# Pausing the gather queue with a short memset, and gathering one group of fields in two blocks: a DLRM tower on one core

## The chip, the cores and the metric

The kernel runs on one core of one Trainium2 chip. The metric is the device time of one execution in microseconds (us), as the median over several runs. Differences of about 1% are what a measurement of this kernel can tell.

## The reference

For 2048 samples, 40 embedding rows of 32 floats are looked up (one table per field, 1000 to 125000 rows each). Every pair of the 40 fields is joined by its own 32x32 matrix (780 pairs), and the 780 results and 16 dense values go through a three-layer perceptron.

```python
e = jnp.stack([tbl_f[ids[:, f]] for f in range(40)], axis=1)            # 2048 x 40 x 32
iidx, jidx = jnp.triu_indices(40, k=1)
z = jnp.einsum('bpd,pde,bpe->bp', e[:, iidx], bilinear_matrices, e[:, jidx])
h = jnp.concatenate([z, dense_ctx], axis=1)                             # 2048 x 796
h = jnp.maximum(h @ W_top1 + b_top1, 0.0)                               # 512
h = jnp.maximum(h @ W_top2 + b_top2, 0.0)                               # 256
y = h @ W_top3                                                          # 2048 x 1
```

## The kernel before

The batch is cut into 4 blocks of 512 samples, the fields into 10 chunks of 4 fields (128 partitions, feature by sample). A block has 50 units, one for each pair of chunks (and five "twin" units for pairs within chunks), and one cycle g works one unit, so the kernel has 200 cycles, 50 for each block. In a cycle TensorE projects a chunk with the pair matrices into PSUM (`project`, L935, L944), VectorE multiplies that with the other chunk (`multiply`, L823 and its like, two multiplications of 128x1024 in a cycle), and TensorE sums the products into `bank_z` (`sum_up`, L960). The sum of cycle g-1 stands behind the projection of cycle g+1 in TensorE's queue.

The embeddings come in two ways.

- Gathered: GpSimd issues indirect DMAs (L586), each of 128 rows of 128 bytes, so 4 for a field and block. They land in `rows`, a ring of 7 slots, one slot for a chunk and block (a "turn"). TensorE transposes the four tiles of a turn (`turn`, L909) once the turn's semaphore has all its landings, and ScalarE copies the result to `x_T` (`keep_turn`, L631). GpSimd goes through the turns in order. It waits for a slot (`turned`), for a due cycle of each field (`DUE`, by `summed`, 0.8 blocks ahead in order), and after every fourth gather (`BURST = 4`) for the landing of the gather just issued (L593).
- Looked up: 16 fields with small tables are multiplied out. Their tables stand in SBUF, split in three bf16 parts. VectorE makes a one-hot matrix of the indices (`one_hot`, L787, 125x2048), TensorE multiplies tables by it (`look`, L886, 12 matmuls for a part, `KC` = 10 parts for a group and block). The fields form four groups; group three (index 2) is fields 16, 9, 34, 23. The indices come by a broadcast DMA on SyncE's queue (`load_wide`, 500 KB). ScalarE copies the result (`keep_look`, L640).

The parts of the lookups for block o+1, and of the perceptron of block o-1 (`mlp`, L987), are spread over the cycles of block o by `place`: one or two parts for a cycle. In block 3 there is no lookup, and the perceptron of block 2 is spread over all its cycles. Behind the last cycle stands the perceptron of block 3 alone.

Before the change the 16 looked-up fields leave 24 fields to gather, 96 gathers for a block, 384 in all, in nine turns for each block. The last turn of a block carries four fields and stands at the block's cycle 37 in block 0 and cycle 36 in the others (cycle 186 of the kernel in block 3).

```python
for t in range(ROWS[o] // P):
    nc.gpsimd.indirect_dma_start(out=rows[:, n % R_SLOTS, t, f, :], ...
        ).then_inc(gathered[n % R_SLOTS], 16)
    begun[n % R_SLOTS] += 1
    if sum(begun) % BURST == 0:
        pool.wait_ge(gathered[n % R_SLOTS], 16 * begun[n % R_SLOTS])
```

Of the kernel before, what the change touches and what calls it, by code (L numbers as in the profile page):

```python
# [12 lines left out]
P = 128  # L13
# [3 lines left out]
CF = P // DIM  # L17
# [6 lines left out]
BLOCKS = len(ROWS)  # L24
# [127 lines left out]
for _r in range(CF):  # L152
# [8 lines left out]
LOOKED = [f for fs in GROUPS for f in fs]  # L161
VOCAB = {36: 1250, 37: 1250, 38: 1000, 39: 1000, 0: 1000, 24: 1000, 2: 1250, 3: 1250, 16: 1250, 9: 1250, 34: 1000,
         23: 1250, 28: 1250, 22: 1250, 30: 1000, 27: 1250}
FIRST_LOOK = [0, 0, 0, 0]
SPLIT_ORDER = [0, 1, 3, 2]


def looks_of(o, J):

    return [q for q, fs in enumerate(GROUPS) if o >= FIRST_LOOK[q] and any(f // CF == J for f in fs)]  # L170


def gathered_fields(o, a):
# [88 lines left out]
for _o in range(1, BLOCKS):  # L262
    _mlp, _next = mlp_jobs(_o - 1), _o + 1 < BLOCKS
    place(_mlp[:2] + [("look", _o + 1, 0)] * _next + _mlp[2:3] + [("look", _o + 1, 1)] * _next + _mlp[3:5]
          + [("look", _o + 1, 3)] * _next + _mlp[5:] + [("look", _o + 1, 2)] * _next,
          FIRST_CYCLE[_o], FIRST_CYCLE[_o + 1] - 1)
for _j in range(RESULTS):
    JOBS.append(("mlp", BLOCKS - 1, _j))
# [1 line left out]
JOB_PARTS = {job: depth(job) for job in JOBS}  # L270
LOOK_ORDER = [job[1:] for job in JOBS if job[0] == "look"]
LOOK_PART = {(o, q, k): n * KC + k for n, (o, q) in enumerate(LOOK_ORDER) for k in range(KC)}
assert all(LOOK_ORDER.index((o, q)) >= 0 for q in range(len(GROUPS)) for o in range(FIRST_LOOK[q], BLOCKS))
SPLIT = {q: n for n, q in enumerate(SPLIT_ORDER)}


# [44 lines left out]
assert all(at + 6 <= g or at == 0 for (o, c, f), at in DUE.items() for g in TURN_AT if (o, c) in TURN_AT[g])  # L321


BURST = 4


U_SLOTS = 3
# [41 lines left out]
def dlrm_tower(nc, dense_ctx, ids, tables, W_top1, b_top1, W_top2, b_top2, W_top3, bil, out):  # L369
    with ExitStack() as ctx:  # L370
        def sb(name, shape, dt=F32):
            return ctx.enter_context(nc.sbuf_tensor(name, shape, dt))
# [40 lines left out]
        y = h2[0:1, 0, :]  # L413
        dense = sb("dense", [P, SUBS, CF, DIM])
        ident = sb("ident", [P, P])
        select = sb("select", [P, 2 * DIM - CF])

        idx_rows = nc.dram_tensor("idx_rows", (NL, BATCH), F16).ap()
# [2 lines left out]
        bank_z = ps("bank_z", [P, NB])  # L421
        misc = ps("misc", [P, NB])

        ids_loaded, ids_rest_loaded = sem("ids_loaded"), sem("ids_rest_loaded")
        W_zeroed, stage_zeroed, W1_zeroed = sem("W_zeroed"), sem("stage_zeroed"), sem("W1_zeroed")
        dense_zeroed = sem("dense_zeroed")
# [55 lines left out]
        @block.sync  # L482
        def _(sp):
            tiles = ids.rearrange("(t p) f -> p t f", p=P)
            sp.dma_start(idx[:, 0:ROWS[0] // P, :], tiles[:, 0:ROWS[0] // P, :]).then_inc(ids_loaded, 16)

            def load_W(c):
                for r, at, p, m in W_LOADS[c]:
                    sp.dma_start(W[r * DIM:(r + 1) * DIM, at:at + m * DIM].rearrange("d (j e) -> d j e", e=DIM),
                                 bil[p:p + m].rearrange("j d e -> d j e")).then_inc(W_landed[c], 16)  # L490

            def load_wide(o, q):
                n = LOOK_ORDER.index((o, q))
                if n > 1:
                    sp.wait_ge(ones_made, (n - 1) * KC)
                sp.dma_start(idx_wide[n % 2][:, 0:len(GROUPS[q]), 0:ROWS[o]],
                             idx_rows[group_cols(q), OFF[o]:OFF[o] + ROWS[o]].partition_broadcast(KP)
                             ).then_inc(wide_landed[n % 2], 16)

            def load_dense(o):  # L500
                if o:
                    sp.wait_ge(summed, FIRST_CYCLE[o])
                for t in range(ROWS[o] // P):
                    sp.dma_start(dense[:, t, :, CF * DENSE_SLOT:],
                                 dense_ctx[OFF[o] + t * P:OFF[o] + t * P + P, :].rearrange("p (r s) -> p r s", s=CF)
                                 ).then_inc(dense_loaded, 16)

            def store_y(o):
                sp.wait_ge(misc_kept, JOB[("mlp", o, RESULTS - 1)] + 1)
                sp.dma_start(out[OFF[o]:OFF[o] + ROWS[o], :].rearrange("n o -> o n"), y[0:1, 0:ROWS[o]]  # L510
                             ).then_inc(y_stored, 16)

            load_tab(sp, 0, 36)
            load_tab(sp, 0, 37)
            sp.wait_ge(stage_zeroed, 1)
            load_tab(sp, 0, 38)
            load_tab(sp, 0, 39)
            sp.dma_start(idx[:, ROWS[0] // P:, :], tiles[:, ROWS[0] // P:, :]).then_inc(ids_rest_loaded, 16)
            for f in GROUPS[1]:
                load_tab(sp, 1, f)  # L520
            sp.wait_ge(W_zeroed, 1)
            load_W(1)
            for f in GROUPS[3]:
                load_tab(sp, 3, f)
            sp.wait_ge(idx_stored, 16)
            load_wide(0, 1)
            load_W(2)
            for f in GROUPS[2]:
                load_tab(sp, 2, f)
            load_wide(0, 3)  # L530
            load_W(3)
            load_wide(0, 2)
            load_W(4)
            load_wide(1, 0)
            load_W(5)
            sp.wait_ge(dense_zeroed, 1)
            load_dense(0)
            load_wide(1, 1)
            load_W(6)
            load_W(7)  # L540
            load_wide(1, 3)
            for c in range(8, CHUNKS):
                load_W(c)
            sp.wait_ge(W1_zeroed, 1)
            for t, row, at, m in W1_LOADS[:len(W1_LOADS) // 2]:
                sp.dma_start(W1[row:row + m, t, :], W_top1[at:at + m, :]).then_inc(mlp_loaded, 16)
            load_wide(1, 2)
            for t, row, at, m in W1_LOADS[len(W1_LOADS) // 2:]:
                sp.dma_start(W1[row:row + m, t, :], W_top1[at:at + m, :]).then_inc(mlp_loaded, 16)

            sp.dma_start(W2[:], W_top2.rearrange("(m p) n -> p m n", p=P)).then_inc(mlp_loaded, 16)
            with nc.allow_non_contiguous_dma(reason="biases and output column, a few values"):
                sp.dma_start(W3[:], W_top3.rearrange("(m p) o -> p (m o)", p=P)).then_inc(mlp_loaded, 16)
                sp.dma_start(b1[:], b_top1.rearrange("(m p) -> p m", p=P)).then_inc(mlp_loaded, 16)
                sp.dma_start(b2[:], b_top2.rearrange("(m p) -> p m", p=P)).then_inc(mlp_loaded, 16)
            for o in range(1, BLOCKS):
                load_dense(o)
                if o + 1 < BLOCKS:
                    for q in (0, 1, 3, 2):
                        load_wide(o + 1, q)  # L560
                store_y(o - 1)
            store_y(BLOCKS - 1)
            sp.wait_ge(y_stored, 16 * BLOCKS)

        @block.gpsimd
        def _(pool):
            nc.gpsimd.memset(ident[:], 0.0).then_inc(ident_made, 1)
            nc.gpsimd.iota(row_of_i[:], pattern=[[1, KC]], base=0, channel_multiplier=KC).then_inc(row_of_made, 1)
            pool.wait_ge(ident_made, 1)
            nc.gpsimd.affine_select(out=ident[:], in_=ident[:], compare_op=ALU.not_equal, fill=1.0, base=0,  # L570
                                    pattern=[[-1, P]], channel_multiplier=1).then_inc(ident_made, 1)
            pool.wait_ge(ids_loaded, 16)
            begun = [0] * R_SLOTS
            for n, (o, c) in enumerate(TURNS):
                if n in (0, 1, 5):
                    pool.wait_ge(rows_zeroed, min(n, 2) + 1)
                if n >= R_SLOTS:
                    pool.wait_ge(turned, n - R_SLOTS + 1)
                for f in GATHERED[(o, c)]:
                    field = CF * CHUNK_OF_STEP[c] + f  # L580
                    if DUE[(o, c, f)]:
                        pool.wait_ge(summed, DUE[(o, c, f)])
                    if n == FIRST_TURN[1] and f == GATHERED[(o, c)][0]:
                        pool.wait_ge(ids_rest_loaded, 16)
                    for t in range(ROWS[o] // P):
                        nc.gpsimd.indirect_dma_start(  # L586
                            out=rows[:, n % R_SLOTS, t, f, :], out_offset=None, in_=tables[field][:, :],
                            in_offset=bass.IndirectOffsetOnAxis(
                                ap=idx[:, OFF[o] // P + t, field:field + 1], axis=0),
                        ).then_inc(gathered[n % R_SLOTS], 16)  # L590
                        begun[n % R_SLOTS] += 1
                        if sum(begun) % BURST == 0:
                            pool.wait_ge(gathered[n % R_SLOTS], 16 * begun[n % R_SLOTS])  # L593

        @block.scalar
        def _(act):
# [278 lines left out]
        def _(pe):  # L875
            def look(o, q, k):
                N, fs = ROWS[o], GROUPS[q]
                n, job = LOOK_PART[(o, q, k)], JOB[("look", o, q)]
                if k == 0 and job:
                    pe.wait_ge(misc_kept, job)  # L880
                if o == FIRST_LOOK[q] and k % (KC // 2) == 0:
                    pe.wait_ge(low_split, 2 * SPLIT[q] + k // (KC // 2) + 1)
                pe.wait_ge(ones_made, n + 1)
                for part in range(3):
# [181 lines left out]
```

## Time and profile before

| | |
|---|---|
| median of 3 runs | 756.91 us |
| lowest and highest run | 754.71 and 761.52 us |
| the profiled execution | 760.99 us |
| its span in the profile | 759.2 us |
| granted TensorE clock, mean | 0.978 |
| gathers (L586) | 384 |

The profile covers one execution. The span runs from the first to the last instruction that it shows; the execution's own time is 1.8 us longer. TensorE is recorded as two rows, PE (the matmuls) and PEld (the weight loads). The clock is given as a share of full speed, 2.4 GHz.

### The profile page before, as it was taken

What the parts mean: (1) busy time and instruction counts of PE and PEld (TensorE: products, weight loads), DVE (VectorE), ACT (ScalarE), POOL (GpSimd) and SP (SyncE); (2) the same over time, 40 slices, a digit from 0 to 9 for tenths busy, and PEclk for the clock granted to TensorE, in tenths of its full rate; (3) what the DMA queues carried; (4) which work ended last, traced back from release to release, by engine and by line L of the source; (5) the groups of instructions that cost most, each with busy time, mean ns of one, the idle gap of its engine ahead of it and who ended that gap; (6) DMA issues with size and microseconds to landing.
All of it is one profiled execution on the core that took longest, in us unless ns stands there. A gap on an engine that the chain in (4) does not pass through costs nothing.

```text
span 759.2 us, 15982 instructions
## 1 busy us (share of the span) xinstructions
PE 710.3 (94%) x6752; PEld 222.8 (29%) x6752; DVE 594.6 (78%) x628; ACT 204.2 (27%) x321; POOL 388.2 (51%) x391
## 2 busy tenths in 40 slices
PE   3878899966999899999999999999999999999998
PEld 2333333312333232323233232322233222222232
DVE  6889899957896588879886798879787877888800
ACT  4362401420232301331414311331414303133002
POOL 5454655555664665555565555555665555550000
PEclk9989999989899899999999999999999999999999
DMA  4444441220003011100002110100001000000000
GB/s 119 115 96 62 76 75 37 59 65 11 10 11 66 11 27 22 33 16 10 11 13 38 38 27 20 31 18 10 11 12 14 11 11 11 11 11 3 1 2 1
DMA packets 62678, 23.28 MB, mean 31 GB/s; under 512 B 45785, under 2 KB 61791, under 8 KB 62607
## 3 DMA queue, kind: packets, MB, share of 16 engines
q1 hardware_dynamic: 50287, 15.88, 8.6%
q0 software_dynamic: 12288, 6.32, 7.2%
q8 instruction: 53, 0.87, 0.5%
q14 instruction: 18, 0.15, 0.1%
q10 hardware_dynamic: 32, 0.07, 0.1%
HBM read 22.15 MB, written 0.07 MB: 29 GB/s over the span
## 4 chain that ended last, share of the span: by engine, by line
PE 54%; POOL 21%; issue 13%; DMA 10%; ACT 2%; DVE 0%; POOLq 0%; ACTq 0%; DVEq 0%
POOL rows L586 21%; PE U L935 15%; PE bank_z L960 15%; DMA rows<-in_tbl,idx 10%; PE misc L987 10%; PE misc L886 7%; PE U L987 4%; PE U L944 2%; PE U L909 2%; ACT x_T L640 1%; ACT x_T L631 0%; PE bank_z L968 0%; DVE prod L823 0%; DMA idx<-in_ids 0%; ACT z L620 0%
## 5 line engine op out<-in xcount | busy, mean ns | idle before, releaser
L586 POOL DMA_INDIRECT rows<-in_tbl,idx x384 | 387.4, 1009 | 296.5 <-DMA rows<-in_tbl,idx 195.3
L823 DVE TENSOR_TENSOR prod<-U,x_T 128x1024 f32<-128x1024 f32 x280 | 329.7, 1218 | 77.4 <-PE U L935 74.6
L960 PE MATMUL bank_z<-prod,select 128*32 128x512 f32 x1600 | 216.0, 612 | 0.7 <-ACT z L620 0.7
L935 PE MATMUL U<-x_T,W 32*128 32x512 f32 x1184 | 185.3, 658 | 8.1 <-ACT x_T L631 5.2
L886 PE MATMUL misc<-ones,tabs 125*32 125x512 bf16 x1920 | 124.7, 393 | 4.2 <-DVE ones L787 3.3
L787 DVE TENSOR_SCALAR ones<-idx_wide,row_of 125x2048 bf16<-125x2048 f16 x160 | 117.0, 755 | 9.8 <-PE misc L886 5.2
L823 DVE TENSOR_TENSOR prod<-U,x_look 128x1024 f32<-128x1024 f32 x80 | 94.8, 1219 | 29.6 <-PE U L935 26.9
L631 ACT ACTIVATE x_T<-U 32x512 f32<-32x512 f32 (+2 forms) x52 | 30.6, 590 | 227.6 <-PE U L909 179.4
L987 PE MATMUL misc<-z,W 128*32 128x512 f32 x728 | 91.8, 597 | 0.0
L935 PEld LDWEIGHTS U<-x_T,W 32*128 32x128 f32 x1184 | 56.0, 188 | 101.3 <-issue 52.0
L886 PEld LDWEIGHTS misc<-ones,tabs 125*32 125x32 bf16 x1920 | 55.9, 99 | 92.1 <-issue 53.0
L960 PEld LDWEIGHTS bank_z<-prod,select 128*32 128x32 f32 x1600 | 31.7, 108 | 156.5 <-issue 91.5
L620 ACT ACTIVATE z<-bank_z 128x512 f32<-128x512 f32 x28 | 16.7, 597 | 106.5 <-PE bank_z L960 91.4
L909 PE MATMUL U<-ident,rows 128*128 128x128 f32 x144 | 24.8, 299 | 19.0 <-DMA rows<-in_tbl,idx 18.3
L935 PE MATMUL U<-x_look,W 32*128 32x512 f32 x256 | 40.7, 640 | 0.0
L987 PEld LDWEIGHTS misc<-z,W 128*32 128x32 f32 x728 | 23.5, 111 | 53.7 <-issue 52.2
L640 ACT ACTIVATE x_T<-misc 32x512 f32<-32x512 f32 (+1 forms) x44 | 25.9, 589 | 33.9 <-PE misc L886 33.4
L987 PE MATMUL misc<-h,W 128*32 128x512 f32 (+1 forms) x204 | 30.1, 593 | 0.8 <-ACT x_T L640 0.8
L658 ACT ACTIVATE x_twin<-x_T 32x512 f32<-32x512 f32 x48 | 30.1, 628 | 1.4 <-issue 0.4
L909 PEld LDWEIGHTS U<-ident,rows 128*128 128x128 f32 x144 | 16.1, 148 | 40.0 <-issue 25.2
L675 ACT ACTIVATE h<-misc,b 128x512 f32<-128x512 f32 x13 | 8.9, 688 | 66.4 <-PE misc L987 66.4
L811 DVE TENSOR_TENSOR prod<-U,x_twin 128x1024 f32<-128x1024 f32 x20 | 24.3, 1214 | 0.0
(66 smaller groups left out, 266.4 us busy)
## 6 DMA issues: line engine op xcount, KB each, us to landing
idx_wide<-idx_rows SPq DMA_DIRECT2D x15, 500.0 KB
rows<-in_tbl,idx POOLq DMA_INDIRECT x384, 2.5
W<-in_W_top SPq DMA_DIRECT2D x100, 8.0 KB
W<-_L_rec_bilinear_matrices SPq DMA_DIRECT2D x72, 16.0 KB, 2.8
prod<-in_tbl SPq DMA_DIRECT2D x4, 156.2 KB
W<-in_W_top SPq DMA_DIRECT2D x35, 2.0 KB
W<-_L_rec_bilinear_matrices SPq DMA_DIRECT2D x4, 128.0 KB
W<-in_W_top SPq DMA_DIRECT2D x1, 512.0 KB
```

The costliest lines, as they stand in the source:

```text
L586: nc.gpsimd.indirect_dma_start(out=rows[:, n % R_SLOTS, t, f, :], out_offset=None, in_=tables[field][:, :], in_offset=bass.IndirectOffsetO ...
L631: last = nc.scalar.activation(x_of(o, J)[lo * DIM:hi * DIM, :], U[lo * DIM:hi * DIM, at, 0:N], ACT.Copy)
L640: last = nc.scalar.activation(x_of(o, J)[lo * DIM:hi * DIM, :], misc[s * DIM:(s + hi - lo) * DIM, 0:ROWS[o]], ACT.Copy)
L658: nc.scalar.activation(x_twin[r * DIM:(r + 1) * DIM, 1, 0:N], x_of(o, a + 1)[(CF - 1 - r) * DIM:(CF - r) * DIM, :], ACT.Copy)
L787: nc.vector.tensor_scalar(ones[:, n % ONES, 0:len(fs), 0:N], idx_wide[job % 2][:, 0:len(fs), 0:N], row_of[0:KP, k:k + 1], None, ALU.is_equ ...
L811: last = nc.vector.tensor_tensor(to[:, :, m * N:(m + 1) * N], U[:, at:at + 2, m * N:(m + 1) * N], x_twin[:, :, 0:N], ALU.mult)
L823: last = nc.vector.tensor_tensor(to[:, :, m * N:(m + n) * N].rearrange("p r (m n) -> p r m n", m=n), U[:, at:at + 2, m * N:(m + n) * N].re ...
L886: last = nc.tensor.matmul(misc[s * DIM:(s + 1) * DIM, 0:N], tabs[0:KP, LOOKED.index(field), part, k * DIM:(k + 1) * DIM], ones[:, n % ONES ...
L909: last = nc.tensor.transpose(U[:, at, t * P:(t + 1) * P], rows[:, n % R_SLOTS, t].rearrange("p f d -> p (f d)"), ident[:])
L935: last = nc.tensor.matmul(U[:, at + r % 2, m * N:(m + 1) * N], W[row, at_W:at_W + P], x_of(o, a)[row, :], start=True, stop=True, skip_grou ...
L960: last = nc.tensor.matmul(bank_z[r * DIM:(r + 1) * DIM, 0:N], sel, prod[:, (2 * g + r // 2) % P_SLOTS, r % 2, m * N:(m + 1) * N], start=(k ...
L987: last = nc.tensor.matmul(bank[part, 0:N], lhs[:, part], rhs, start=(t == 0), stop=(t == depth - 1), skip_group_check=True)
```

## The change

- `LOOK_BLOCKS` takes the place of `FIRST_LOOK`. Group three is looked up in blocks 0 and 1 only. In blocks 2 and 3 its four fields (16, 9, 34, 23) are gathered, as part of turns that exist already: 28 fields and 112 gathers in each of these blocks, 416 in all. The 20 lookup parts of the two blocks are gone, with their one-hot matrices and two index broadcasts, and `place` spreads what is left anew.
- `BURST` is 2. Behind every second gather GpSimd writes a memset over a tile `pause` of 128x448 bytes and waits for that memset, in place of the wait for the fourth gather's landing. There are 208 such pauses.

```diff
-FIRST_LOOK = [0, 0, 0, 0]
+LOOK_BLOCKS = [BLOCKS, BLOCKS, 2, BLOCKS]
 def looks_of(o, J):
-    return [q for q, fs in enumerate(GROUPS) if o >= FIRST_LOOK[q] and any(f // CF == J for f in fs)]
+    return [q for q, fs in enumerate(GROUPS) if o < LOOK_BLOCKS[q] and any(f // CF == J for f in fs)]
...
-          + [("look", _o + 1, 3)] * _next + _mlp[5:] + [("look", _o + 1, 2)] * _next,
+          + [("look", _o + 1, 3)] * _next + _mlp[5:] + [("look", _o + 1, 2)] * (_o + 1 < LOOK_BLOCKS[2]),
...
-BURST = 4
+BURST = 2
...
+        pause = sb("pause", [P, 448], mybir.dt.uint8)
...
+        paused = sem("paused")
...
                     for q in (0, 1, 3, 2):
-                        load_wide(o + 1, q)
+                        if o + 1 < LOOK_BLOCKS[q]:
+                            load_wide(o + 1, q)
...
-            begun = [0] * R_SLOTS
+            begun, pauses = [0] * R_SLOTS, 0
...
                         if sum(begun) % BURST == 0:
-                            pool.wait_ge(gathered[n % R_SLOTS], 16 * begun[n % R_SLOTS])
+                            pauses += 1
+                            nc.gpsimd.memset(pause[:], 0).then_inc(paused, 1)
+                            pool.wait_ge(paused, pauses)
...
-                if o == FIRST_LOOK[q] and k % (KC // 2) == 0:
+                if o == 0 and k % (KC // 2) == 0:
```

## Rows read from the trace of the kernel before

**Rows 1.** The page, part 1: busy time of each engine, share, instructions.

```profile
PE 710.3 (94%) x6752; PEld 222.8 (29%) x6752; DVE 594.6 (78%) x628; ACT 204.2 (27%) x321; POOL 388.2 (51%) x391
```

**Rows 2.** The waits: who waited for whom, us in total, times, longest.

```profile
POOL rows L586 <- DMA rows<-in_tbl,idx: 195.3, 89, 5.9
...
POOL rows L586 <- issue: 87.8, 288, 0.3
...
PE U L909 <- DMA rows<-in_tbl,idx: 18.3, 7, 6.0
...
POOL rows L586 <- PE bank_z L960: 10.1, 5, 2.8
```

**Rows 3.** The timeline of TensorE, transposes that waited, in time order.

```profile
88.79 0.89 PE L909 MATMUL U<-ident,rows 128*128 128x128 f32 x4 [2.01 <-DMA rows<-in_tbl,idx]
...
161.33 1.09 PE L909 MATMUL U<-ident,rows 128*128 128x128 f32 x4 [5.46 <-DMA rows<-in_tbl,idx]
...
189.38 1.09 PE L909 MATMUL U<-ident,rows 128*128 128x128 f32 x4 [5.97 <-DMA rows<-in_tbl,idx]
...
260.12 1.08 PE L909 MATMUL U<-ident,rows 128*128 128x128 f32 x4 [2.77 <-DMA rows<-in_tbl,idx]
...
531.59 0.63 PE L909 MATMUL U<-ident,rows 128*128 128x128 f32 x4 [0.68 <-DVE prod L823]
...
686.78 0.63 PE L909 MATMUL U<-ident,rows 128*128 128x128 f32 x4 [0.32 <-DMA rows<-in_tbl,idx]
```

**Rows 4.** Stretches of block 0, and one of block 2.

```profile
120.00:140.00 20.00, 19.20 (x216) 6.18 (x212) 18.94 (x21) 7.53 (x13) 9.99 (x10) 1.00 0.27 53
140.00:160.00 20.00, 15.87 (x140) 4.50 (x136) 16.67 (x16) 2.95 (x5) 11.36 (x12) 1.00 0.20 46
160.00:180.00 20.00, 17.99 (x116) 5.36 (x116) 13.97 (x13) 5.58 (x9) 10.22 (x11) 0.83 0.23 49
180.00:200.00 20.00, 14.03 (x90) 4.11 (x88) 11.51 (x12) 4.68 (x8) 12.28 (x13) 0.83 0.08 11
...
460.00:500.00 40.00, 40.00 (x412) 11.95 (x408) 34.93 (x37) 9.86 (x16) 22.54 (x23) 1.00 0.13 24
```

**Rows 5.** The timeline of TensorE in block 2, beside lookups.

```profile
479.87 1.48 PE L886 MATMUL misc<-ones,tabs 125*32 125x512 bf16 x24
481.28 1.14 PE L935 MATMUL U<-x_T,W 32*128 32x512 f32 x8
```

**Rows 6.** The timeline of GpSimd, four gathers of block 3.

```profile
674.21 0.95 POOL L586 DMA_INDIRECT rows<-in_tbl,idx  x1 [1.67 <-DMA rows<-in_tbl,idx]
675.46 0.95 POOL L586 DMA_INDIRECT rows<-in_tbl,idx  x1 [0.30 <-issue]
...
680.59 0.95 POOL L586 DMA_INDIRECT rows<-in_tbl,idx  x1 [1.68 <-DMA rows<-in_tbl,idx]
```

**Rows 7.** The chain that ended last: start, us, what.

```profile
677.96 2.37 DMA rows<-in_tbl,idx
684.34 2.31 DMA rows<-in_tbl,idx
```

**Rows 8.** The timeline of GpSimd's first instructions.

```profile
0.25 0.10 POOL L1055 MEMSET const-float32-0.0<- 128x1 f32 x1 [0.25 <-issue]
0.28 0.10 POOL L1055 MEMSET const-float32-1.0<- 128x1 f32 x1
...
0.74 0.20 POOL L567 MEMSET ident<- 128x128 f32 x1 [0.29 <-POOLq L1055]
```

**Rows 9.** Gathers and one-hots in the timelines of GpSimd and VectorE.

```profile
40.54 2.98 POOL L586 DMA_INDIRECT rows<-in_tbl,idx  x1 [3.19 <-DMA rows<-in_tbl,idx]
...
474.34 1.37 POOL L586 DMA_INDIRECT rows<-in_tbl,idx  x1 [0.30 <-issue]
...
474.15 0.74 DVE L787 TENSOR_SCALAR ones<-idx_wide,row_of 125x2048 bf16<-125x2048 f16 x1
```

**Rows 10.** The page, part 5: costliest groups, by line.

```profile
L586 POOL DMA_INDIRECT rows<-in_tbl,idx x384 | 387.4, 1009 | 296.5 <-DMA rows<-in_tbl,idx 195.3
L823 DVE TENSOR_TENSOR prod<-U,x_T 128x1024 f32<-128x1024 f32 x280 | 329.7, 1218 | 77.4 <-PE U L935 74.6
...
L787 DVE TENSOR_SCALAR ones<-idx_wide,row_of 125x2048 bf16<-125x2048 f16 x160 | 117.0, 755 | 9.8 <-PE misc L886 5.2
```

More of the change, by code:

```diff
@@ L272 @@
 LOOK_PART = {(o, q, k): n * KC + k for n, (o, q) in enumerate(LOOK_ORDER) for k in range(KC)}
-assert all(LOOK_ORDER.index((o, q)) >= 0 for q in range(len(GROUPS)) for o in range(FIRST_LOOK[q], BLOCKS))
+assert all(LOOK_ORDER.index((o, q)) >= 0 for q in range(len(GROUPS)) for o in range(LOOK_BLOCKS[q]))
 SPLIT = {q: n for n, q in enumerate(SPLIT_ORDER)}
```

## The prediction

> **What bounds the kernel now.** I read the busy shares first: TensorE is busy 94% of the span, GpSimd 51% [rows 1]. That alone would make GpSimd look idle, so I went on to the waits. GpSimd spends 195.3 us waiting for its own gathers to land and 87.8 us in short gaps between gathers, and only 10.1 us for its due cycles [rows 2]. 387.4 us of gathers [rows 10] and these waits fill its time without a break from its first gather at 3.2 us to its last, whose landing begins at 684.34 us [rows 7]. So there are two long chains, side by side. GpSimd's queue is one, TensorE's the other, and they meet at the transposes. There the timeline shows TensorE waiting for landings in block 0 and at the start of block 1: seven waits, 18.3 us [rows 2], the large ones 5.46 us at 161.33 and 5.97 us at 189.38 [rows 3]. From there to 687 TensorE is ahead of need and busy all the time (40.00 of 40 us in block 2 [rows 4]). The last transpose that needs a gather, at 686.78 us, again waits, 0.32 us [rows 3]. There the two chains end together; 72.4 us follow (759.2 - 686.8) in which nothing is gathered. An edit that shortens only one of the chains gains in block 0 and little more. The change touches both.
>
> **TensorE's chain, the waits for gathers.** A faster gather queue removes them. What is late next in block 0 is VectorE: it was busy 18.94 of 20 us in the stretch ahead of the large waits, and 16.67, 13.97 and 11.51 in the three that hold them [rows 4]. That is 17.85 us idle; at the 1.06 us for 20 us of the stretch ahead, 3 us of it stay, and 15 us are to be had. Part of it is the clock: 0.83 of 2.4 GHz was granted over two of these stretches, so part of them ran at 1.2 GHz, after TensorE had stood still, and the transposes take 1.09 us there and 0.63 later [rows 3]. The three small waits ahead of that (2.01 us at 88.79 the largest [rows 3]) lie where VectorE sets the pace; I count 2 us. The wait at 260.12 lies where TensorE sets the pace: 2.77 us [rows 3] and about 2 us of slow work behind it, 5 us. Together 22 us, between 15 (the large ones alone) and 27 (all DVE idle, and the rest doubled for the clock).
>
> **TensorE's chain, the lookups.** 20 parts of 12 matmuls go. Two parts take 481.28 - 479.87 = 1.41 us of TensorE's queue [rows 5], so 0.70 each, 14 us, in the cycles of blocks 1 and 2, where TensorE has no idle time [rows 4]. The 20 one-hots take 20 x 0.755 = 15 us from VectorE [rows 10], which had 5 us to spare in 40 [rows 4]: it stays hidden. Where a cycle now holds a single lookup part and a one-hot, VectorE can be the later one (two multiplications of 1.218 and 0.755 [rows 10] make 3.2 us), and I give back 2 us. No transpose is added, since the turns exist; ScalarE (27% busy [rows 1]) loses eight copies; SyncE's queue loses two broadcasts. All of this costs nothing, and none of it ends a wait. TensorE's chain: 759.2 - 22 - 14 + 2 = 725 us, from 718 to 735.
>
> **GpSimd's chain.** It gets 32 more gathers and, for 96 landing waits, 208 pauses. Its work is: start 3.2; gathers 387.4 + 32 x 1.009 = 419.7 [rows 10]; between the two gathers of a pair 0.30 us as now [rows 6], 208 x 0.30 = 62.4; the last landing, 2.3 from its gather's start less the 0.95 counted, 1.4 [rows 6, 7]; the part behind it 72.4. That is 559 us. To it come 207 pauses of length p, each from the end of one gather to the start of the next. So T = 559 + 207 p, and everything hangs on p. At p = 0.80 the chain is as long as TensorE's 725; at 0.97 it is 759.2, no change. Now the four gathers to a wait take 6.4 us (680.59 - 674.21 [rows 6]), 1.60 each; in the new form they take 1.01 + 0.15 + p/2.
>
> No row shows a pause, so I bound it. The memset: 0.10 us for one element, 0.20 for 128 of them [rows 8], 0.8 ns an element. If bytes count as elements, 448 take 0.46 us. If four bytes go as one, 112 take 0.19 us. I take 0.46, the only form that the rows show being by elements. Before it: the first memsets follow each other at 0.03 us [rows 8], and after a gather every next one comes 0.30 us late [rows 6]. The low end is 0, the high end 0.30. Behind it: the gather that waits for a landing starts 680.59 - 677.96 - 2.37 = 0.26 us after the landing [rows 6, 7], and that includes the semaphore. I take that from both ends. So p lies between 0.19 + 0.26 = 0.45 and 0.46 + 0.30 + 0.26 = 1.02. I take 0.05 for the gap in front, since the 0.30 looks like the start of a gather (0.26 of it stands behind a landing too), and 0.06 for memsets that meet a one-hot. p = 0.83, T = 559 + 172 = 731 us.
>
> That contact with one-hots is in the rows: the gather at 474.34 took 1.37 us, not 0.95, beside a one-hot that started at 474.15 [rows 9]. Over all gathers the excess is 384 x (1.009 - 0.95) = 23 us, 0.14 for each of the 160 one-hots.
>
> The Trainium skill has this in "SBUF — State Buffer", section "SBUF: two separate sides", in the box on DVE blocking a software-generated DMA: while VectorE runs in a two-port mode, GpSimd is locked out and cannot write descriptors. The trace agrees with it by the 1.37 us. By this rule the 20 one-hots that go would give the gathers 20 x 0.14 = 3 us back, and the sum would be 728.
>
> **Where gathers catch up.** The pace matters in block 3 alone. In the middle, the last turn of block 2 needs 304 gathers, at 1.57 each by 482 us. That cycle comes about 33 us before its present time of 531.6 us [rows 3], so GpSimd is ahead by 16. The due cycles hold it back little, since it is nowhere earlier than now by more than it is needed. The landing waits' own excess (up to 5.9 us each [rows 2], where broadcasts and weights go through the same engines) no longer stops the queue. It costs only if a turn is due just then.
>
> **Rivals.**
> 1. The pause is short (p under 0.72). Then TensorE's chain alone is left, 718 to 727 us in the span. For it speaks a memset of 0.19 us; against it that 448 bytes would be an odd way to write a short one.
> 2. Slower: the gap of 0.30 us is the tail of a gather, on the GpSimd cores that issued it, and the memset must wait for it, and then the next gather's start comes on top. This is p = 1.02 or more, T = 559 + 211 = 770 us, and the loss shows in block 3, at whose last turn every gather of the kernel must have landed. It decides from p = 0.97. For it speaks that the gap is 0.30 after each of 288 gathers [rows 2]; against it, that a start after a landing has nearly the same 0.26. The Trainium skill, "Perfetto Trace Analysis", section "DMA Instruction — SWDGE (GPSIMD)", says that the recorded end is that of the last descriptor, and that the core completes its program after it; no row here shows that tail.
> 3. Gathers lengthen when nothing waits for their landing, because more of them are under way. The 2.98 us gather at 40.54 [rows 9], amid weight loads, speaks for it; the even 0.95 of block 3, with one or two under way, against. 0.1 us for each of 416 gathers is 42 us: 773 us.
> 4. The change does not do what it says: the pause takes the landing wait's place with no gain in pace (p near 0.93 to 0.97), and TensorE's 36 us are lost again at the turns of block 3. 752 to 760 us.
>
> **How the numbers follow.** Forecast (p from 0.72 to 0.92): 0.50, span 725 to 750. Rival 1: 0.20. Rival 2: 0.12. Rival 3: 0.07. Rival 4: 0.11. The likeliest is 731 us of span, plus the 1.8 us around it, 733 of the profiled execution's 761.0; the median of the runs lies 4.1 us under that execution, so 729. The range reaches to rival 1 below and over rival 4 above: 714 to 764. About 1% is what a measurement of this kernel can tell. Faster by more: forecast, rival 1 and a little of rival 4, 0.73. Within it: most of rival 4 and the lower part of rival 2, 0.12. Slower: 0.15.
>
> **What would show it.** In the profile of the changed kernel: memsets of 0.46 us, gathers of 0.95 to 1.01 us with 0.3 between, and 0.77 to 0.9 from one pair to the next; no wait of a transpose from 60 to 260 us, with the clock whole there; block 3's last transpose at about 658 us, with GpSimd working until just before it or with a wait of a few us for the landing; GpSimd's waits for due cycles still small. Transposes of block 3 that wait for landings by 10 us and more mean rival 2 or 4; mean gathers over 1.1 us mean rival 3; a GpSimd that stands at due cycles or slots, and ends early, means rival 1. The forecast is wrong if p is, since 0.1 us of it is 21 us; if VectorE, not the gathers, held block 0 back, the 15 us there are wrong.

## The result, and the profile after

The changed kernel takes 729.6 us (median of 4 runs, 727.9 to 731.2) beside 757.8 for the kernel before (4 runs): ratio 0.9625, 95% interval 0.9574 to 0.9676. Its profiled execution took 728.7 us, its span is 726.9. Two later comparisons gave 0.9612 (0.9541 to 0.9682) and 0.964 (0.9599 to 0.9681).

The page of the changed kernel: part 1, three rows of part 2 (the span in 40 slices), and groups of part 5.

```profile
PE 693.9 (95%) x6512; PEld 215.8 (30%) x6512; DVE 597.1 (82%) x608; ACT 197.1 (27%) x309; POOL 522.2 (72%) x631
...
PE   2767999999999999999999999999999999999998
...
POOL 7888888888887888888887888888888887830000
PEclk9999999999999999999999999999999999999999
...
L589 POOL DMA_INDIRECT rows<-in_tbl,idx x416 | 410.2, 986 | 121.3 <-issue 63.5
...
L792 DVE TENSOR_SCALAR ones<-idx_wide,row_of 125x2048 bf16<-125x2048 f16 x140 | 119.0, 872 | 7.0 <-ACT idx_wide L691 3.4
...
L597 POOL MEMSET pause<- 128x448 uint8 x208 | 111.7, 537 | 0.1
```

GpSimd's idle time ahead of gathers fell from 296.5 us [rows 10] to 121.3, with 32 gathers more. The memsets cost 111.7 us. One row goes the wrong way: a one-hot takes 0.872 us on average, not 0.755 [rows 10]. So VectorE is busy 2.5 us longer than before (597.1 beside 594.6 [rows 1]), although 20 one-hots are gone.

The stretches of the changed kernel, to be laid beside [rows 4] (PE, PEld, DVE, ACT, POOL busy, the clock, DMA share, GB/s):

```profile
140.00:160.00 20.00, 19.31 (x160) 5.79 (x152) 18.28 (x18) 7.31 (x12) 15.96 (x22) 1.00 0.21 49
160.00:180.00 20.00, 20.00 (x150) 5.88 (x142) 18.98 (x19) 5.58 (x9) 16.27 (x21) 1.00 0.25 49
180.00:200.00 20.00, 19.98 (x182) 6.89 (x184) 20.00 (x21) 1.24 (x3) 16.24 (x20) 1.00 0.08 12
```

TensorE is busy and its granted clock is 1.00, the 2.4 GHz, where it waited and was granted 0.83 over two of the stretches before; VectorE has 2.7 us idle there, not 17.9. The timeline of TensorE, with the transposes that answer to four of [rows 3] (cycles 29, 37, 57 and 186):

```profile
154.57 0.66 PE L914 MATMUL U<-ident,rows 128*128 128x128 f32 x4
174.36 0.66 PE L914 MATMUL U<-ident,rows 128*128 128x128 f32 x4
...
240.15 0.66 PE L914 MATMUL U<-ident,rows 128*128 128x128 f32 x4
...
654.45 0.66 PE L914 MATMUL U<-ident,rows 128*128 128x128 f32 x4
```

None of them waits for a landing any more. They come 6.8, 15.0, 20.0 and 32.3 us earlier. The transposes of cycle 63, in the timelines of the kernel before and of the changed one:

```profile
283.03 0.66 PE L909 MATMUL U<-ident,rows 128*128 128x128 f32 x4
```

```profile
260.23 0.66 PE L914 MATMUL U<-ident,rows 128*128 128x128 f32 x4
```

So the gain is made in two parts: about 23 us by cycle 63, and the other 9.5 us between there and cycle 186. The last gathers of the kernel, in GpSimd's timeline:

```profile
640.68 0.49 POOL L597 MEMSET pause<- 128x448 uint8 x1
641.44 0.95 POOL L589 DMA_INDIRECT rows<-in_tbl,idx  x1 [0.27 <-POOL pause L597]
642.70 0.95 POOL L589 DMA_INDIRECT rows<-in_tbl,idx  x1 [0.30 <-issue]
```

From one pair to the next it is 0.49 of memset and 0.27 behind it. The last landing is at about 645 us (642.7 + 0.95 + 1.4), 9 us ahead of its transpose. The chain that ended last now says the same: TensorE has 89% of it and GpSimd no line.

```profile
PE 89%; DVE 5%; ACT 4%; DMA 1%; issue 1%; ACTq 0%; DVEq 0%
```

### The profile page after: what moved, and what is told of

Same layout as the page of the kernel before. It is cut to its first block, busy times and chain, and to the rows that moved or that the text cites. A ratio compares the mean times of both kernels' runs of the same rounds, so it can differ in the third digit from the quotient of the medians.

```text
span 726.9 us, 15700 instructions
## 1 busy us (share of the span) xinstructions
PE 693.9 (95%) x6512; PEld 215.8 (30%) x6512; DVE 597.1 (82%) x608; ACT 197.1 (27%) x309; POOL 522.2 (72%) x631
## 4 chain that ended last, share of the span: by engine, by line
PE 89%; DVE 5%; ACT 4%; DMA 1%; issue 1%; ACTq 0%; DVEq 0%
PE U L940 28%; PE bank_z L965 26%; PE misc L992 14%; PE misc L891 10%; PE U L992 4%; PE U L949 3%; DVE ones L792 3%; PE U L914 3%; ACT x_T L645 1%; DMA idx_wide<-idx_rows 1%; DVE prod L828 1%; ACT x_twin L663 1%; PE bank_z L973 0%; DVE tabs L779 0%; ACT x_twin L666 0%
## 5 line engine op out<-in xcount | busy, mean ns | idle before, releaser
L589 POOL DMA_INDIRECT rows<-in_tbl,idx x416 | 410.2, 986 | 121.3 <-issue 63.5
L965 PE MATMUL bank_z<-prod,select 128*32 128x512 f32 x1600 | 213.1, 604 | 0.7 <-ACT z L625 0.7
L792 DVE TENSOR_SCALAR ones<-idx_wide,row_of 125x2048 bf16<-125x2048 f16 x140 | 119.0, 872 | 7.0 <-ACT idx_wide L691 3.4
L891 PE MATMUL misc<-ones,tabs 125*32 125x512 bf16 x1680 | 108.4, 388 | 7.3 <-DVE ones L792 5.3
L597 POOL MEMSET pause<- 128x448 uint8 x208 | 111.7, 537 | 0.1
L940 PEld LDWEIGHTS U<-x_T,W 32*128 32x128 f32 x1184 | 57.8, 183 | 102.9 <-issue 49.4
L636 ACT ACTIVATE x_T<-U 32x512 f32<-32x512 f32 (+2 forms) x48 | 28.3, 591 | 188.8 <-PE U L914 115.0
L891 PEld LDWEIGHTS misc<-ones,tabs 125*32 125x32 bf16 x1680 | 47.4, 98 | 85.0 <-issue 46.0
L645 ACT ACTIVATE x_T<-misc 32x512 f32<-32x512 f32 (+1 forms) x36 | 21.2, 589 | 68.1 <-PE misc L891 67.7
L949 PE MATMUL U<-x_T,W 32*64 32x512 f32 x160 | 24.1, 612 | 1.2 <-ACT x_twin L673 1.2
```

Of the source, the lines that this page charges most:

```text
L597: nc.gpsimd.memset(pause[:], 0).then_inc(paused, 1)
L636: last = nc.scalar.activation(x_of(o, J)[lo * DIM:hi * DIM, :], U[lo * DIM:hi * DIM, at, 0:N], ACT.Copy)
L645: last = nc.scalar.activation(x_of(o, J)[lo * DIM:hi * DIM, :], misc[s * DIM:(s + hi - lo) * DIM, 0:ROWS[o]], ACT.Copy)
L792: nc.vector.tensor_scalar(ones[:, n % ONES, 0:len(fs), 0:N], idx_wide[job % 2][:, 0:len(fs), 0:N], row_of[0:KP, k:k + 1], None, ALU.is_equ ...
L891: last = nc.tensor.matmul(misc[s * DIM:(s + 1) * DIM, 0:N], tabs[0:KP, LOOKED.index(field), part, k * DIM:(k + 1) * DIM], ones[:, n % ONES ...
L940: last = nc.tensor.matmul(U[:, at + r % 2, m * N:(m + 1) * N], W[row, at_W:at_W + P], x_of(o, a)[row, :], start=True, stop=True, skip_grou ...
```

## The experiments

These are twelve runs of eight kernels, on four chips. The kernel before took 757.8 us beside the result, 761.8 on the chip of e5 to e8 and 757.9 on that of e12, but 813.7 us on that of e1 to e4 and 796.2 us on that of e9 to e11. On these two, engines stand still at places where the profile names nothing that they wait for ("issue") or only "remote" (another core or a queue that it doesn't know). I call them stalling chips. A time from there stands only beside others from the same chip. Each chip was seen in one session alone, so a passing condition of that session, and not the chip, isn't excluded as the cause.

**e1 and e10: the new lookups alone, with landing waits.**

```diff
-BURST = 2
+BURST = 4
-                            pauses += 1
-                            nc.gpsimd.memset(pause[:], 0).then_inc(paused, 1)
-                            pool.wait_ge(paused, pauses)
+                            pool.wait_ge(gathered[n % R_SLOTS], 16 * begun[n % R_SLOTS])
```

> Only the second part of the change: group three is gathered in blocks 2 and 3, but GpSimd waits for the landing of every fourth gather as before. If GpSimd's queue is a chain of its own, its length is 3.2 + 416 gathers of 1.009 (419.7) + 312 gaps of 0.30 (93.6) + 103 landing waits of 2.18 (224.5, the mean of the 95 of before) + 1.4 + 72.4 = 815 us of span, 7% slower than before, with the last transposes of blocks 2 and 3 waiting for landings. If TensorE's chain alone sets the time, it is 759.2 - 14 = 745 us.

> As e1, repeated: the new lookups alone, with landing waits. e1's own sum was 815; what it measured was 797.4 us of span with GpSimd at work throughout, the mean landing wait 2.05 us rather than 2.18. If GpSimd's chain is the bound, it is 797 us again on any chip, since nothing in it depends on the other engines: 5% slower than before where before takes 760. If TensorE's chain were the bound, 745.

Measured: e1 799.6 us (before 813.7, ratio 0.984, 0.975 to 0.993), span 797.4; e10 799.5 us (before 796.2, ratio 1.0045, 0.9992 to 1.0099), span 798.8. Both fell on stalling chips. GpSimd's row in e1:

```profile
L589 POOL DMA_INDIRECT rows<-in_tbl,idx x416 | 415.7, 999 | 304.7 <-DMA rows<-in_tbl,idx 191.0 <-issue 94.8 <-PE bank_z L963 15.3
```

From its first gather at 3.2 us it works and waits for 415.7 + 302.9 us (304.7 less the 1.8 ahead of that first gather); with 1.4 for the last landing and the 72.4 us behind it that is 795.6, against 797.4. The transposes of cycle 186 wait 2.5 us for the last landing in e1, so GpSimd's chain is what binds there. Two chips with different times for the kernel before gave the same 799.5, as such a bound should. The expectation of e10 that nothing in the chain depends on the other engines doesn't hold quite: 15.3 us in e1 and 6.5 in e10 are waits for due cycles, which TensorE sets (and 191.0 and 203.4 are landing waits), so that the two times are so equal is in part chance. The sum of 815 was 2% too high: it has a mean landing wait of 2.18 us (measured 2.05) and 103 of them (93 show in e1). The new lookups by themselves lengthen GpSimd's chain and would lose on a chip where before takes 760; that last step is argued, as no run of this kernel fell on one.

**e2 and e6: the pauses alone, all lookups kept.**

```diff
-LOOK_BLOCKS = [BLOCKS, BLOCKS, 2, BLOCKS]
+LOOK_BLOCKS = [BLOCKS, BLOCKS, BLOCKS, BLOCKS]
```

> Only the first part: the memset pauses, with all four groups looked up in every block (384 gathers). TensorE's chain loses its waits for landings and keeps the 20 lookup parts: 759.2 - 22.8 (what the transpose of block 1's cycle 63 had gained in the changed kernel) = 736 us of span, 3% faster than before and 1.3% slower than the changed kernel. GpSimd is done with its 384 gathers by about 600 us or is held by due cycles. If the pause were the whole gain, it would come out at 727 like the changed kernel.

> As e2, repeated beside the changed kernel: pauses alone, all lookups kept. Where no stalls of the kind 'issue' and 'remote' are seen, 736 us of span: 3% faster than before and 1.3% slower than the changed kernel. Where they are seen, slower than before, as in e2, and still slower than the changed kernel beside it by the 20 lookup parts, 14 us or more.

Measured: e2, on the stalling chip, 838.4 us, ratio 1.035 (1.027 to 1.042). e6 749.5 us, ratio 0.985 (0.978 to 0.992), beside e5's 731.3. So the pauses alone bring 12.4 us of the 761.8, and the lookups behind them another 18.2. The expected 736 of span missed: e6's span is 748.3. The expected distance to the changed kernel, 1.3% or some 9 us, missed too; it is 2.5%. Its row for one-hots shows where time was lost:

```profile
L792 DVE TENSOR_SCALAR ones<-idx_wide,row_of 125x2048 bf16<-125x2048 f16 x160 | 139.4, 894 | 9.3 <-PE misc L891 4.5
```

160 one-hots at 0.894 us and not 0.755: 22 us more work for VectorE. The transposes of cycles 63 and 186 in e6:

```profile
268.14 0.66 PE L914 MATMUL U<-ident,rows 128*128 128x128 f32 x4
...
675.84 0.66 PE L914 MATMUL U<-ident,rows 128*128 128x128 f32 x4
```

**e3 and e8: no pause and no wait.**

```diff
                         if sum(begun) % BURST == 0:
                             pauses += 1
-                            nc.gpsimd.memset(pause[:], 0).then_inc(paused, 1)
-                            pool.wait_ge(paused, pauses)
```

> The changed kernel without memset and without wait: GpSimd issues gathers back to back, 1.25 to 1.29 us each, or stands at due cycles and slots. If TensorE's chain sets the time (my reading of the changed profile: the last landing is 9 us ahead of its transpose), nothing is gained by it: 727 us of span, within 0.5%. If the one-hots of VectorE slow down beside a denser stream of gathers and that matters, it is 1 to 2% slower. If gathers lengthen when more of them are under way (the prediction's third rival), their mean is over 1.1 us and TensorE waits for landings in block 3: 740 us or more.

> As e3, repeated beside the changed kernel, to see whether the loss is of the chip or of the kernel. If of the kernel: 12 to 20% slower than the changed kernel on any chip, with matmuls of a lookup issued one by one, up to 2.2 us apart, while gathers follow each other without a break. If only the chip of e3 does it: the changed kernel's time within 0.5%.

Measured: e8 722.1 us, ratio 0.949 (0.942 to 0.956), 9 us faster than the changed kernel beside it; e3, the same kernel on a stalling chip, 925.4 us, ratio 1.142 (1.134 to 1.151). So neither alternative of e8 held: the kernel without a pause is the faster one on one chip and by far the slowest on another. e8's groups of part 5:

```profile
L589 POOL DMA_INDIRECT rows<-in_tbl,idx x416 | 424.8, 1021 | 144.2 <-issue 118.5
...
L790 DVE TENSOR_SCALAR ones<-idx_wide,row_of 125x2048 bf16<-125x2048 f16 x140 | 104.3, 768 | 8.4 <-ACT idx_wide L689 3.4
```

The gathers' mean is 1.02 us with nothing that holds them back (1.00 in e3), beside 1.01 before and 0.99 in the changed kernel. The 0.1 us for each of the prediction's third rival is not there, on either chip. The one-hots are back at 0.77. The same two transposes in e8:

```profile
256.12 0.66 PE L912 MATMUL U<-ident,rows 128*128 128x128 f32 x4
...
647.54 0.66 PE L912 MATMUL U<-ident,rows 128*128 128x128 f32 x4
```

In e3 this is what stands still, in the timelines of TensorE and GpSimd:

```profile
48.55 0.59 PE L889 MATMUL misc<-ones,tabs 125*32 125x512 bf16 x1 [2.21 <-issue]
51.35 0.59 PE L889 MATMUL misc<-ones,tabs 125*32 125x512 bf16 x1 [2.21 <-issue]
54.16 0.59 PE L889 MATMUL misc<-ones,tabs 125*32 125x512 bf16 x1 [2.21 <-issue]
```

```profile
49.97 0.94 POOL L589 DMA_INDIRECT rows<-in_tbl,idx  x1 [0.30 <-issue]
51.22 0.95 POOL L589 DMA_INDIRECT rows<-in_tbl,idx  x1 [0.31 <-issue]
52.47 0.95 POOL L589 DMA_INDIRECT rows<-in_tbl,idx  x1 [0.30 <-issue]
```

While GpSimd issues a gather every 1.25 us, TensorE issues one matmul of a lookup every 2.8 us, and the profile names no semaphore that it waits for. VectorE's waits in e3, with the totals by what ended them:

```profile
DVE prod L826 <- remote: 57.9, 24, 6.1
DVE ones L790 <- remote: 51.9, 13, 20.9
...
DVE ones L790 <- issue: 23.8, 2, 19.7
```

In e8 VectorE's waits name no "remote" at all. Slower DMA packets are not what the profile shows: those that load instructions (q8: 51 packets, 0.84 MB in both) took 0.5% of the DMA engines' time in e8's span of 720.0 us and 0.4% in e3's of 915.8, and those of the gathers 9.2% and 6.4%.

**e4: a second pause.** Made to test the sum for GpSimd's chain.

```diff
                             nc.gpsimd.memset(pause[:], 0).then_inc(paused, 1)
                             pool.wait_ge(paused, pauses)
+                            pauses += 1
+                            nc.gpsimd.memset(pause[:, 0:128], 0).then_inc(paused, 1)
+                            pool.wait_ge(paused, pauses)
```

> A second memset of 128 bytes and a wait for it behind each pause. It adds 0.2 us of memset and 0.05 to 0.3 us around it, so p grows from 0.80 by 0.25 to 0.5. By the sum for GpSimd's chain, whose length in the changed kernel was 717.5 us (last landing at 645.1 plus 72.4 behind it), the span is 717.5 + 207 x 0.25 to 0.5 = 769 to 821 us, 1 to 8% slower than before. If GpSimd had much more slack than 9 us, or the tail behind the last turn shrank, it would be less, down to 727.

Measured: 808.8 us, ratio 0.9995 (0.9953 to 1.0037), span 805.4. The span lies in the expected 769 to 821; "1 to 8% slower than before" doesn't hold, since the kernel before took 813.7 there. The groups of GpSimd, and its wait for the pause:

```profile
L589 POOL DMA_INDIRECT rows<-in_tbl,idx x416 | 410.9, 988 | 145.4 <-POOL pause L600 76.9 <-issue 66.8 <-DMA idx<-in_ids 1.8
L597 POOL MEMSET pause<- 128x448 uint8 x208 | 108.9, 524 | 0.1
L600 POOL MEMSET pause<- 128x128 uint8 x208 | 52.5, 252 | 12.0
```

p is 0.52 + 0.25 + 0.06 + 0.37 = 1.20 us, and the prediction's sum, with these gathers and gaps, is 3.2 + 410.9 + 66.8 + 1.4 + 72.4 + 207 x 1.20 = 803, against 805.4. TensorE waits 55.2 us for landings, the last time by 3.5 us at cycle 186. So the chain is shown as the bound at p = 1.20; the slope of 207 us for each us of p is the number of pauses, and only this one longer pause tested it. This was a stalling chip, yet the kernel shows few unexplained stops (6 us of "issue" on TensorE's matmuls, 15 on VectorE, no "remote").

**e5 and e12: the changed kernel again.**

> The changed kernel itself, beside its parts. In the first four experiments the kernel before took 813.7 us, not 757.8, and every kernel with a dense stream of gathers showed matmuls and multiplications that stood still for nothing that the profile names ('issue' and 'remote': 2 us in the changed kernel's own first profile, 44 us on TensorE's matmuls and on VectorE 75 us or more in the two fastest gather streams). If that is a matter of the chip and of how densely GpSimd issues, the changed kernel shows such stalls here too wherever the kernel before is slow, and its ratio to the kernel before is then worse than 0.9625. If the ratio is 0.96 again, the stalls hit both alike.

> The changed kernel itself once more. Two of four chips so far showed a kernel before of 796 to 814 us with engines that stand still for 'issue' and 'remote', and there every kernel with landing waits replaced was slower than before by 3.5 to 18%, more so the denser its gathers. If this run falls on such a chip: gathers at 1.43 us each lie between those of e4 (1.6, ratio 0.9995) and e2 (1.43 in block 0, ratio 1.035, with 20 more lookup parts), so a ratio between 0.99 and 1.03, the gain of the change gone. If it falls on a chip where the kernel before takes 755 to 766: 0.961 again.

Measured: 731.3 us (before 761.8) and 731.4 us (before 757.9), ratios 0.961 and 0.964. Neither fell on a stalling chip, so what the change does there was not seen. e2 (1.035) and e4 (0.9995) are its neighbours.

**e7: a memset of 32 bytes.**

```diff
-        pause = sb("pause", [P, 448], mybir.dt.uint8)
+        pause = sb("pause", [P, 32], mybir.dt.uint8)
```

> The memset shrunk from 448 to 32 bytes. It takes 0.13 us (0.10 and 0.8 ns an element), so p falls from 0.80 to about 0.43 and a pair of gathers to 2.7 us. If TensorE's chain alone sets the time, the changed kernel's time within 0.5%. If density of the gathers is what makes the other engines stand still, it lies between the changed kernel and the one without a pause: 3 to 12% above the changed kernel, with more 'issue' idle time on TensorE and VectorE.

Measured: 722.3 us, ratio 0.949 (0.941 to 0.956). It is 9.0 us (1.2%) faster than the changed kernel, outside the 0.5% of the first theory and on the other side from the second. The wait for the memset is there as before, only its length is gone. e7's groups:

```profile
L792 DVE TENSOR_SCALAR ones<-idx_wide,row_of 125x2048 bf16<-125x2048 f16 x140 | 103.0, 758 | 10.6 <-PE misc L891 3.6
```

One-hots at 0.758. So it is the 448 bytes that cost, by VectorE. The timelines of VectorE and of GpSimd in e5 show a single case:

```profile
406.51 1.13 DVE L792 TENSOR_SCALAR ones<-idx_wide,row_of 125x2048 bf16<-125x2048 f16 x1
```

```profile
406.61 0.49 POOL L597 MEMSET pause<- 128x448 uint8 x1
407.37 1.09 POOL L589 DMA_INDIRECT rows<-in_tbl,idx  x1 [0.27 <-POOL pause L597]
```

The one-hot started at 406.51, the memset 0.10 us behind it, and the one-hot took 1.13 us in place of 0.74. In e5's trace the one-hot starts first in 25 such overlaps. In 10 of them the memset keeps its 0.49 and the one-hot takes 1.13 to 1.34 us; in the other 15 the memset takes 0.92 to 1.03 us, and the one-hot 0.74 to 1.21.

**e9 and e11: more gathers without a pause, and no pause with the old lookups.**

```diff
-LOOK_BLOCKS = [BLOCKS, BLOCKS, 2, BLOCKS]
+LOOK_BLOCKS = [BLOCKS, BLOCKS, 1, 2]
-place([("look", 1, 2)], FIRST_CYCLE[1] - 10, FIRST_CYCLE[1])
...
-    place(_mlp[:2] + [("look", _o + 1, 0)] * _next + _mlp[2:3] + [("look", _o + 1, 1)] * _next + _mlp[3:5]
-          + [("look", _o + 1, 3)] * _next + ...
+    place(_mlp[:3] + [("look", _o + 1, 0)] * _next + _mlp[3:4] + [("look", _o + 1, 1)] * _next + _mlp[4:5]
+          + [("look", _o + 1, 3)] * (_o + 1 < LOOK_BLOCKS[3]) + ...
...
-            load_wide(1, 2)
...
-                            nc.gpsimd.memset(pause[:], 0).then_inc(paused, 1)
-                            pool.wait_ge(paused, pauses)
```

> A candidate beyond both kernels: no pause at all, group three looked up in block 0 only, and group four (fields 28, 22, 30, 27) in blocks 0 and 1 only; in block 1 and 2 the perceptron's third and fourth result stand ahead of the second lookup. 464 gathers. TensorE's chain: 720.0 (the span without a pause, e8) less 30 lookup parts of 0.70 = 699 us. GpSimd's chain: 3.2 + 464 x 1.021 + 463 x 0.30 + 1.4 + 72.4 = 690 us. So 699 to 704 us of span if the gathers keep up and no engine stands still for 'issue'; 14% or more slower than before where the other engines stall beside dense gathers, as in e3.

> No wait for landings and no memset, all lookups kept: TensorE's chain with its 18.3 us of waits for gathers taken away and nothing put in their place. The prediction's term for that is 22 us (15 to 27): 738 us of span, against the 748.3 of e6 with the memsets. The difference to e6 is what the memsets cost VectorE's one-hots (0.894 us each in e6, 0.755 in the kernel before). If the memsets cost nothing, it is 748 like e6.

e11 is e3 with `LOOK_BLOCKS` as in e2. Measured: e9 940.2 us, ratio 1.176 (1.160 to 1.192); e11 888.6 us, ratio 1.120 (1.109 to 1.130). Both fell on a stalling chip, so the sums of 699 and 738 us were not tested. What they add: a second and third kernel without a pause lose 12 to 18%, on a second chip. Their waits are as in e3 (in e11 one stop of TensorE for "issue" is 46.5 us long).

## Why the prediction was right, and where not

The time was forecast at 729 and measured at 729.6. The terms behind it are less good than that, and that it came so near is luck. The span was forecast at 731 and is 726.9. The 4.1 us that the forecast took off, as the distance of the median from the profiled execution, made up for that by chance: in the changed kernel the median is 0.9 us above the profiled execution.

*The chain that binds was the wrong one of two.* The forecast took GpSimd's chain, 731 us, with TensorE's 6 us behind at 725. Measured, TensorE's is 726.9 and GpSimd's 717.5 (last landing at 645.1, and the 72.4 us behind it). The form of GpSimd's sum held: with the measured values it gives 3.2 + 410.2 + 62.4 + 1.4 + 72.4 + 207 x 0.81 = 717. The pause was sized at p = 0.83 and is 0.81: 0.54 of memset, against 0.52 with the meeting of one-hots, and 0.27 behind, against 0.26, and no gap in front, against 0.05. What was mis-sized are the gathers, 0.986 us and not 1.009, 9.5 us in all.

*The waits of TensorE: 22 us.* Without the 448-byte memsets the transpose of cycle 63 comes 25.7 us (e7) and 26.9 us (e8) earlier than in the trace of the kernel before, which is from another chip; by that, 22 was 4 to 5 too small. With them it comes 22.8 us earlier in the changed kernel's first trace, 19.5 and 18.9 in e5 and e12, and 14.9 in e6. That part of the sum left out what the memsets cost VectorE: it had the meeting with one-hots as 0.06 us of p and nothing for the one-hots. Up to cycle 57 TensorE's work is the same in all these kernels, and the transpose of that cycle comes later the longer the one-hots ahead of it took. The 81 or 82 that start before it add up to 60.9 and 61.8 us in e7 and e8 (transpose at 237.5 and 236.1), to 68.4, 68.1 and 71.2 in the three traces of the changed kernel (240.2, 243.2 and 243.7), and to 74.2 in e6 (248.3). So TensorE's 725 us is two errors that cancel: its waits were worth more than 22, and the 7 to 9 us that the slower one-hots cost (spans of 726.9 and 729.4 beside e8's 720.0) were put at nothing.

*The lookups: 14 less 2, 12 us.* From cycle 63 to 186 the kernel before takes 403.8 us, and e7 and e8 take 391.4: 12.3 us less, as forecast. The changed kernel takes 394.2 (393.5 in e5, 394.4 in e12), 2 to 3 us more than e8, again beside slower one-hots. e6, with the old lookups and the memsets, takes 407.7. So of the 18.2 us between e5 and e6, 14.2 lie behind cycle 63 and 4.6 ahead of it (18.8 in the traces), where 5.1 stood already at cycle 57, before the first cycle whose lookup parts differ. That VectorE's share stays hidden holds in e7 and e8, and not quite where memsets slow the one-hots.

*The rivals.* That the pause be short (p under 0.72) and that gathers lengthen both fell. But what rival 1 would have brought, TensorE's chain alone and 718 to 727 us of span, is what came, at p = 0.81: GpSimd's chain was 13.5 us shorter than forecast, 9.5 of them by its gathers. The tail of a gather, which would delay the memset, isn't there: the memset starts within 0.01 us of the gather's recorded end. The change's pace did not turn out to be that of the landing wait (rival 4). The rule of the Trainium skill ("SBUF — State Buffer", "SBUF: two separate sides") that GpSimd is locked out while VectorE runs in a two-port mode was held to be worth 3 us of gather time, outside of the sum. The lengthened memsets agree with it (0.92 to 1.03 us in place of 0.49). The 3 us don't show: with all 160 one-hots e6's gathers take 0.988 us, with 140 the changed kernel's take 0.986. And the loss that counted runs the other way: it is VectorE's one-hot that is held up beside GpSimd's memset, by up to 0.6 us.

*What the pause is for* the prediction did not ask, and this is the largest gap. On a chip without stalls the 448 bytes are a loss: a pause of 32 bytes (e7) and none (e8) are both 1.2% faster. On the stalling chips the kernels without a pause lose 12 to 18% to the one before, one with 448 bytes and the old lookups loses 3.5%, and one with 576 bytes and the new ones loses nothing. In these five the denser GpSimd issues its gathers where nothing holds it, the more the other engines stand still: 1.25 us for a gather in e3, e9 and e11, 1.48 in e2's pairs, 1.6 to 1.75 in e4's. The mean pace isn't all of it: e1, on the chip of e4 and at about the same 1.6 to 1.7 us for a gather (four in a row 1.25 apart, then the landing wait), has 44 us of "remote" on VectorE, and e4 has none. That would fit the density within a burst, but no run tests it by itself. Which path the engines share is open: neither the profile nor any run here names it.

## What to carry to other kernels

Add up the chain of each engine that works without a break, its own waits included, and compare the sums: a queue that is busy half the time can be as long as the engine that is busy 94%, and a change to one of them gains only until the other is reached. A wait that is replaced by dummy work isn't free for others: look at what the dummy shares with its neighbours (here 9 us of VectorE's one-hots), and try it at almost no length. Read a gain stretch by stretch in several traces: the total came out right here while its terms were wrong in opposite directions. And measure a change to the density of DMAs on more than one chip before believing it: the same kernel gave 722 us on one and 925 on another.

## What the runs showed of the hardware that was not expected

- A memset of 128x448 bytes on GpSimd takes 0.49 us alone and 0.92 to 1.03 where a one-hot of VectorE (tensor_scalar, f16 to bf16, SBUF to SBUF) holds it up; the one-hot takes 0.74 alone and up to 1.34 (e5). With 32 bytes the one-hots' mean is 0.758, with 448 it is 0.864 (e7, e5).
- A GpSimd memset of bytes goes by elements: 32 bytes in a partition take 0.14 us and 448 take 0.49 (medians of e7 and e5), 0.83 ns a byte.
- A gather behind a wait for a memset starts 0.27 us after the memset's end, a gather behind a gather 0.30, a memset behind a gather within 0.01.
- On two of the four chips of these runs the kernel before is 5 to 7% slower, and on one of them the densest gather stream by 28% (e8 to e3), with TensorE, VectorE and ScalarE stopped for "issue" and "remote".
